# A four-stage transformer block on one core: other buffers and placements for the feed-forward halves, the distances of the first attention and the projections

## The chip, the core and the metric

The kernel runs on one core of a Trainium2 chip. A core has five engines with queues of their own: PE (TensorE, matmuls into PSUM), DVE (VectorE), ACT (ScalarE), POOL (GpSimd) and SP (SyncE, which here issues all DMAs). They meet through semaphores alone, and each takes its instructions strictly in the order in which they are written. The metric is device time in microseconds.

## The reference

The input x is 8 x 1024 x 256, float32. Four layers follow each other, each a residual one over a layer norm (LN):

```python
x = x + attn_a(layernorm(x))   # distance attention
x = x + ffn(layernorm(x))
x = x + attn_b(layernorm(x))   # softmax attention, 16 heads of 16
x = x + ffn(layernorm(x))

# attn_a: V = LN @ wv.T + bv; pos = LN @ w3d.T + b3d          (three coordinates)
#         attn = softmax over k of -|pos_q - pos_k| / 4, causal, the same for all heads
#         out = (attn @ V) @ wo.T + bo
# attn_b: k, q, v = LN @ Wkqv + bkqv; softmax(q k / 4), causal; out = attn @ v
# ffn:    x_prev = x one token back (zero at the first)
#         xr = mu_r * x + (1 - mu_r) * x_prev;  xk likewise
#         out = sigmoid(xr @ W_r.T) * (relu(xk @ W_k.T) ** 2 @ W_v.T)
```

## The kernel before

The program has one backbone and work hung beside it. The backbone is the second attention (att3). A batch element has 4 groups of 4 heads, a group has 12 pieces, a piece has 4 quarters, one for each head: 48 quarters a group, 192 an element (TURN). In quarter u (`pe_att3`, L797 to L841) PE computes one scores piece into one of two max_banks (L811), from which DVE takes the row maxima (L867 with the causal mask, L870 without), and, for the piece 14 slots (56 quarters) earlier, the transposed scores into one of two exp_banks (L822), which ACT exponentiates into pt (L852). POOL clears the part above the diagonal (L889), and once in four quarters PE multiplies with the values into o_bank (L837). At a group's end the maxima go through a side bank and a DMA back into the stack (L910, L920, L929), and halves of the output go through ot, a transposition (L944), a division (L954, L958) and an addition on POOL (L968).

The scores need exact products, so keys and queries are split into three bfloat16 parts, stored to DRAM (L702) and loaded back as stacks ks and qs, nine DMAs a group (L772). The first group of an element can be loaded once all eight parts of that element are stored.

Everything else is a stage: `att1` (first attention), `ffn2`, `proj3` (keys, queries and values of the second attention), `ffn4`. Each stage has an LN for each half h of 512 tokens. STAGES gives a starting quarter to every stage; offsets inside a stage come from JOBS and from `at(...)`. In turn n - 1 of the backbone the stages att1, ffn2 and proj3 of element n run, and ffn4 of element n - 2. All side jobs of PE use three PSUM banks (side): `place()` walks through the quarters, gives each job a bank and a quarter (PARTS_AT), and the quarter where it is emptied (EMPTIED_AT); where no bank is free the job is late, and all later ones keep that shift, which falls by one for 4 quarters. `WRITTEN_AT` applies the same shift to what is placed by `at`. `schedule` then writes, for each engine, the instructions quarter by quarter: those of att3 first, then those of the stages in the order of their start. A quarter is thus an order, no time; an engine that waits holds up all that is written behind it.

The first attention (att1): values with positions (L516, L389), positions turned into rows (L524, L439), then 12 pieces of distances: squares of three coordinate differences on ACT (L451), sums on POOL (L505) and DVE (L405), logarithm and two exponentials on ACT (L465, L468, L473), a select on POOL (L494), and one attend job for each tile of queries (L544) with the division and the residual on DVE (L412, L415). PIECE_TIME gives the quarters of a piece. In `dve_att1` residual and distance share one list: the residual that is due at a piece stands before that piece's L405.

The feed-forward halves: difference to the previous token on POOL (L559), two mixes on DVE (L582, L589), keys (L644), relu (L610), square (L567), receptance (L658), the sigmoid as exponential, logarithm, exponential on ACT (L619, L623, L626), products (L658), multiplication (L599), addition (L572). Their buffers are borrowed: xr, xk, ka lie in pb, kr and th in sq, both buffers of the distances. So ffn2 of an element waits for its last distance (L556, p1_exp), and the distances of the next element wait for the last feed-forward half (tm_ready). Both halves of a stage follow each other, since the second needs the first's last token, which lies beside it in xt.

An LN is statistics on DVE (L330, L337, L340), a power on POOL (L347), four normalisations on POOL (L353), transpositions on PE (L379) and copies to xt on ACT (L368). proj3 has eight projections (L718) into x32 (L687), split by DVE (L671, L674, L678) and POOL (L694).

Before quarter 0 stand the stages of element 0 (FIRST), where nothing of att3 runs beside them.

## Time and profile before

| | us |
|---|---|
| median of 3 runs | 2153.86 (2149.85 to 2161.84) |
| the profiled execution | 2155.86 |
| its span | 2154.1 |
| granted TensorE clock, mean | 0.941 of full speed |

The 2 us between the span and the time lie outside the instructions. The span falls into a prologue up to the first scores matmul (201.9 us), turns 0 to 7 of att3's 192 quarters, and a drain after the last scores matmul (2063.6). The windows of the rows below are cut at the scores matmul that begins a turn, or a stretch of quarters in a turn; those inside a turn are of turn 4, which begins at 1161.6 us. A busy engine is one with an instruction running; two that overlap count once, so the mean duration of an instruction times its count can be more than the busy time.

### The profile page before, as it was taken

To read this page: it belongs to the slowest core of one execution; us is meant where nothing else is said; L and a number is where in the kernel's file an instruction comes from. 1 tells how busy PE (TensorE), PEld (TensorE's weight loads), DVE (VectorE), ACT (ScalarE), POOL (GpSimd) and SP (SyncE) were. 2 spreads that over 40 slices of the span, in tenths; PEclk is the share of its full clock that TensorE was granted. 3 is DMA by queue.
4 is the path that set the end of the run, shared out by engine and by line. 5 is a ranking of instruction groups with operands and counts; after the bars stand their busy time and mean duration, and the time that the engine had idled before them with its cause. 6 is when DMAs were issued, how large, how long until landed. Compare 5 with 4: busy or idle time off the path is not lost. (4 is left out here: it accounts for less than half of the span.)

```text
span 2154.1 us, 32514 instructions
## 1 busy us (share of the span) xinstructions
PE 1852.8 (86%) x9842; PEld 921.0 (43%) x9842; DVE 1427.4 (66%) x4173; ACT 1245.4 (58%) x2673; POOL 1027.3 (48%) x1074
## 2 busy tenths in 40 slices
PE   4476799889998899988998899978998899988986
PEld 3344344434543355434544345424554345323423
DVE  2235767766786677776776676776876677777732
ACT  0722655685648655595557755495557756465562
POOL 4364254436662465435753366534753357314314
PEclk8778699999999999999999999999999999999988
DMA  3006010211223111311123111311123102322000
GB/s 103 1 8 140 1 31 23 67 30 30 40 88 60 31 30 55 74 31 30 41 74 74 30 21 49 89 31 30 31 77 79 24 11 40 98 47 44 1 21 20
DMA packets 64348, 97.27 MB, mean 45 GB/s; under 512 B 15656, under 2 KB 58030, under 8 KB 58031
## 3 DMA queue, kind: packets, MB, share of 16 engines
q1 hardware_dynamic: 64174, 95.20, 20.1%
q8 instruction: 80, 1.31, 0.3%
q14 instruction: 94, 0.76, 0.1%
HBM read 61.09 MB, written 33.55 MB: 44 GB/s over the span
## 5 line engine op out<-in xcount | busy, mean ns | idle before, releaser
L852 ACT ACTIVATE pt<-exp_bank 128x512 f32<-128x512 f32 (+3 forms) x1536 | 748.2, 496 | 664.7 <-PE exp_bank L822 657.5
L867 DVE CUSTOM_DVE_ANT_0 max_bank<-max_bank,mask 128x128 f32<-128x128 f32 (+3 forms) x1024 | 501.4, 501 | 402.1 <-PE max_bank L811 387.7
L811 PE MATMUL max_bank<-ks,qs 96*128 96x512 bf16 (+3 forms) x1536 | 517.9, 342 | 81.4 <-DVE piece_max L870 45.0
L822 PE MATMUL exp_bank<-qs,ks 98*128 98x512 bf16 (+3 forms) x1536 | 512.6, 340 | 69.2 <-ACT pt L852 67.0
L870 DVE TENSOR_REDUCE piece_max<-max_bank 128x1 f32<-128x512 f32 x512 | 343.5, 685 | 105.6 <-PE max_bank L811 102.3
L837 PE MATMUL o_bank<-pt,v 128*17 128x512 f32 (+3 forms) x3072 | 335.6, 510 | 7.6 <-ACT pt L852 3.1
L353 POOL TENSOR_SCALAR xh<-xs,mv,rstd 128x256 f32<-128x256 f32 x256 | 321.2, 1261 | 10.0 <-PE side L379 3.8
L811 PEld LDWEIGHTS max_bank<-ks,qs 96*128 96x128 bf16 x1536 | 150.6, 98 | 382.7 <-DVE piece_max L870 136.5
L889 POOL TENSOR_SCALAR_AFFINE_SELECT pt<-pt 128x512 f32<-128x512 f32 x256 | 170.4, 666 | 291.6 <-ACT pt L852 291.3
L822 PEld LDWEIGHTS exp_bank<-qs,ks 98*128 98x128 bf16 x1536 | 151.9, 100 | 281.4 <-ACT pt L852 174.6
L505 POOL TENSOR_TENSOR sq<-sq 128x512 f32<-128x512 f32 (+1 forms) x96 | 95.9, 999 | 230.1 <-ACT sq L451 230.1
L544 PE MATMUL side<-vp,p 128*128 128x260 f32 x576 | 169.6, 419 | 29.2 <-ACT p L473 19.5
L451 ACT ACTIVATE sq<-pb,neg_pos 128x512 f32<-128x512 f32 (+3 forms) x288 | 179.9, 627 | 2.4 <-ACT p L473 0.4
L644 PE MATMUL side<-pb,wkT 128*128 128x512 f32 x256 | 146.5, 664 | 9.7 <-DVE pb L582 9.6
L867 DVE DVE_READ_ACCUMULATOR2_ANT piece_max<- 128x1 f32 x1024 | 144.5, 141 | 0.0
L968 POOL TENSOR_TENSOR xs<-xs,on 128x256 f32<-128x256 f32 x64 | 49.4, 772 | 186.6 <-DVE on L958 186.6
L544 PEld LDWEIGHTS side<-vp,p 128*128 128x128 f32 x576 | 107.9, 203 | 68.3 <-ACT p L473 34.6
L718 PE MATMUL side<-xt,wkq 128*128 128x512 f32 x256 | 135.4, 615 | 1.5 <-DVE v L743 0.8
L559 POOL TENSOR_TENSOR pb<-xt 128x512 f32<-128x512 f32 x64 | 66.2, 1042 | 143.9 <-PE side L658 123.9
L658 PE MATMUL side<-wrT,pb 128*128 128x256 f32 x512 | 133.9, 387 | 0.0
L658 PE MATMUL side<-wvT,pb 128*128 128x256 f32 x512 | 133.1, 386 | 0.0
L379 PE MATMUL side<-ident,xh 128*128 128x128 f32 x512 | 84.1, 292 | 53.8 <-POOL xh L353 48.5
(94 smaller groups left out, 2284.0 us busy)
## 6 DMA issues: line engine op xcount, KB each, us to landing
parts_dram<-parts SPq DMA_DIRECT2D x64, 384.0 KB, 2.6
qs<-parts_dram SPq DMA_DIRECT2D x192, 128.0 KB, 7.1
ks<-parts_dram SPq DMA_DIRECT2D x32, 384.0 KB, 4.7
xs<-in_L_attn_a_x_dram SPq DMA_DIRECT2D x16, 512.0 KB, 4.2
ks<-parts_dram SPq DMA_DIRECT2D x32, 256.0 KB, 5.4
out_dram<-xs SPq DMA_DIRECT2D x16, 512.0 KB, 3.0
ks<-parts_dram SPq DMA_DIRECT2D x32, 128.0 KB, 5.9
qs<-neg_maxT SPq DMA_DIRECT2D x64, 8.0 KB, 1.9
```

Source lines behind the costliest of these rows:

```text
L353: pool.tensor_scalar(xh[:, t, :], src[:, TPH * h + t, :], mv[:, r, t, 0:1], rstd[:, r, t:t + 1], ALU.subtract, ALU.mult).then_inc(xh_ready, 1)
L451: mm = act.activation(sq[:, p % 2, c, 0:w], pb[:, c, q0:q1], ACT.Square, bias=neg_pos[:, kt, c:c + 1])
L544: mm = pe.matmul(bank[:, 0:VC], p1[:, at:at + P], vp[:, kt, :], start=(kt == 0), stop=(kt == t))
L644: mm = pe.matmul(bank[:, :], wkT[:, c, P * j:P * (j + 1)], xk[:, c, :], start=(c == 0), stop=(c == NC - 1))
L658: mm = pe.matmul(bank[:, C * t:C * (t + 1)], lhs[:, c, P * (2 * j + t):P * (2 * j + t + 1)], rhs[:, c, :], start=(c == 0), stop=(c == NC - 1))
L811: pe.matmul(max_bank[u % MAX_BANKS][:, 0:k1 - k0], qs[r][0:KROWS, j, P * tile:P * (tile + 1)], ks[r][0:KROWS, j, k0:k1], start=True, stop= ...
L822: pe.matmul(exp_bank[k % EXP_BANKS][:, 0:q1 - q0], ks[r][:, j, P * kt:P * (kt + 1)], qs[r][:, j, q0:q1], start=True, stop=True).then_inc(s ...
L837: mm = pe.matmul(o_bank[32 * j:32 * j + VW, q0 - HALF * h:q1 - HALF * h], v3[n % 2][:, kt, GH * (g % NG) + j, :], pt[:, (e - 1) % 2, j, 0: ...
L852: act.activation(pt[:, e % 2, j, 0:q1 - q0], exp_bank[k % EXP_BANKS][:, 0:q1 - q0], ACT.Exp, scale=SCALE).then_inc(exp_done, 1)
L867: dve.tensor_tensor_reduce(scores, scores, mask[:, HALF - w:HALF], 1.0, LOWEST, ALU.add, ALU.max, piece_max[:, j, m:m + 1]).then_inc(max_f ...
L870: dve.tensor_reduce(piece_max[:, j, m:m + 1], scores, AX.X, ALU.max).then_inc(max_free, 1)
L889: pool.affine_select(out=block, in_=block, compare_op=ALU.is_ge, fill=0.0, base=0, pattern=[[0, GH], [1, P]], channel_multiplier=-1).then_ ...
```

## The change

- xk, xr, ka and th become buffers of their own; kr and tm are gone (relu writes ka, the square and the product are done in place). x32 and parts move into p1 instead, so the projections wait for p1's last attend matmul, and p1's first exponential of the next element for the stored parts. ot has one buffer.
- ffn2 and ffn4 alternate by halves: ffn4 0, ffn2 0, ffn4 1, ffn2 1 at quarters 38, 56, 74, 92 of a turn (before 82, 50, 98, 66). ACT keeps the last column of each first half in `edge` and puts it back before the second half.
- The distances take 80 quarters (8 for a piece of 512) instead of 60. In `dve_att1` values, distances and residuals become three lists, so a distance no longer stands behind a residual.
- Projections and values of proj3 get quarters of their own (PROJECT_AT, VALUES_AT), in two groups of four.
- For element 0 DVE normalises in POOL's place.
- A delay falls by one for 3 quarters.

```diff
-ATT1, FFN2, FFN4, PROJ3 = -44, 50, 82, 114
-FIRST = {("att1", 0): -220, ("ffn2", 0): -126, ("proj3", 0): -74,
-         ("att1", 1): -28, ("ffn2", 1): 66, ("proj3", 1): 114}
+STARTS = {("att1", 0): -36, ("att1", 1): -24, ("ffn4", 0): 38, ("ffn2", 0): 56, ("ffn4", 1): 74, ("ffn2", 1): 92,
+          ("proj3", 0): 108, ("proj3", 1): 138}
+HEAD = -200
-LN_HALF = {"att1": 8, "ffn2": 16, "ffn4": 16, "proj3": 12}
...
-PIECE_TIME = [2 + (q1 - q0) // P for _, q0, q1 in KEY_PIECES] + [5, 5, 5]
-PIECE_AT = [34 + sum(PIECE_TIME[:p]) for p in range(NP + 4)]
+PIECE_TIME = [{P: 4, 2 * P: 5, 3 * P: 7, 4 * P: 8}[q1 - q0] for _, q0, q1 in KEY_PIECES] + [5, 5, 5]
+PIECE_AT = [32 + sum(PIECE_TIME[:p]) for p in range(NP + 4)]
...
+PROJECT_AT = [18, 22, 26, 30, 46, 49, 52, 55]
+VALUES_AT = [34, 37, 57, 59]
...
-            regained = max(0, shift - max(0, at - before) // 4)
+            regained = max(0, shift - max(0, at - before) / REGAIN)
...
-        xr, xk, ka = (pb[:, k, :].rearrange("p (c n) -> p c n", c=NC) for k in range(3))
-        kr = sq[:, 0, 0:2, :]
-        th = sq[:, 1, 0:2, :].rearrange("p a (b c) -> p (a b) c", c=C)
-        tm = sb("tm", [P, TPH, C])
-
-        x32 = sb("x32", [P, 2, HALF])
-        parts = sb("parts", [P, 2, 3, HALF], BF16)
+        xk, xr, ka = (sb(name, [P, NC, HALF]) for name in ("xk", "xr", "ka"))
+        th = sb("th", [P, TPH, C])
+        edge = sb("edge", [P, 2, NC, 1])
+
+        x32 = p1[:, 0:2 * HALF].rearrange("p (r n) -> p r n", r=2)
+        parts = p1[:, 2 * HALF:5 * HALF].bitcast(BF16).rearrange("p (r k n) -> p r k n", r=2, k=3)
...
+            if n > 0:
+                return
+            for t in range(TPH):
+                yield at(7 + t)
...
+                dve.tensor_scalar(xh[:, t, :], src[:, TPH * h + t, :], mv[:, r, t, 0:1], rstd[:, r, t:t + 1],
+                                  ALU.subtract, ALU.mult).then_inc(xh_ready, 1)
...
+                    if h == 1 and s in ("ffn2", "ffn4"):
+                        act.wait_ge(edge_kept, EDGE_AT[s, n] + 1)
+                        act.activation(last, kept, ACT.Copy).then_inc(edge_put, 1)
...
+            if h == 0 and s in ("ffn2", "ffn4"):
+                act.wait_ge(xt_ready, 2 * q + 2)
+                act.activation(kept, last, ACT.Copy).then_inc(edge_kept, 1)
...
-                    if s == "ffn2":
-                        pool.wait_ge(p1_exp, NP * (n + 1))
                     if f > 0:
                         pool.wait_ge(r_full, 2 * f)
+                    if h == 1:
+                        pool.wait_ge(edge_put, EDGE_AT[s, n] + 1)
...
                 if f > 0:
-                    act.wait_ge(ka_ready, 2 * f - 1 + j)
-                act.activation(kr[:, j, :], side_of("keys", s, n, h, j)[:, :], ACT.Relu).then_inc(kr_ready, 1)
+                    act.wait_ge(v_full, 2 * f)
+                act.activation(ka[:, j, :], side_of("keys", s, n, h, j)[:, :], ACT.Relu).then_inc(kr_ready, 1)
...
-                        act.wait_ge(tm_ready, 2 * f - 1 + j)
+                        act.wait_ge(x_added, 2 * f - 1 + j)
...
+                if j == 0:
+                    act.wait_ge(pv1_full, 8 * (n + 1))
```

Three places show how the order moves. First POOL in the prologue, from the end of the distances of element 0 to its projections. xh is the normalised half, pb (xr after) the difference, pb<-sq (ka<-ka after) the square, xs the addition, parts (p after) the split of a projection. Before:

```order
L347 TENSOR_TENSOR rstd<-var_eps,minus_half 128x4
L353 TENSOR_SCALAR xh<-xs,mv,rstd 128x256 x4
L567 TENSOR_TENSOR pb<-sq 128x512 x2
L559 TENSOR_TENSOR pb<-xt 128x512 x2
L572 TENSOR_TENSOR xs<-xs,tm 128x512 x2
L567 TENSOR_TENSOR pb<-sq 128x512 x2
L572 TENSOR_TENSOR xs<-xs,tm 128x512
L347 TENSOR_TENSOR rstd<-var_eps,minus_half 128x4
L572 TENSOR_TENSOR xs<-xs,tm 128x512
L353 TENSOR_SCALAR xh<-xs,mv,rstd 128x256 x4
```

After:

```order
L590 TENSOR_TENSOR xs<-xs,th 128x512
L579 TENSOR_TENSOR xr<-xt 128x512 x2
L362 TENSOR_TENSOR rstd<-var_eps,minus_half 128x4
L585 TENSOR_TENSOR ka<-ka 128x512 x2
L712 TENSOR_TENSOR p<-p 128x512
L590 TENSOR_TENSOR xs<-xs,th 128x512 x2
L712 TENSOR_TENSOR p<-p 128x512 x3
L362 TENSOR_TENSOR rstd<-var_eps,minus_half 128x4
L712 TENSOR_TENSOR p<-p 128x512 x4
```

The normalisations are gone from POOL, and the first split of a projection stands ahead of the second half's last additions.

Second DVE in a turn, where the last distance piece (L405, L435 after, 128 columns) meets the residual of a tile (L412 and L415, L445 and L448 after). L867 and L885 are maxima of att3. Before, at quarter 53:

```order
L867 ISA max_bank,piece_max<-max_bank,mask 128x256
L867 ISA piece_max 128x1
L412 RECIPROCAL rinv<-side 128x1
L415 SCALAR_TENSOR_TENSOR xs<-side,rinv,xs 128x256
L405 SCALAR_TENSOR_TENSOR sq<-sq 128x128
L330 BN_STATS st<-xs 128x6
```

After, at quarters 81 and 82:

```order
L435 SCALAR_TENSOR_TENSOR sq<-sq 128x128
L335 BN_STATS st<-xs 128x6
L885 ISA max_bank,piece_max<-max_bank,mask 128x128
L885 ISA piece_max 128x1
L445 RECIPROCAL rinv<-side 128x1
L448 SCALAR_TENSOR_TENSOR xs<-side,rinv,xs 128x256
```

The distance stands ahead of the residual, and 28 quarters later.

Third PE near a turn's end, at the last projection of an element (L718, L736 after), whose parts the next turn's stack is made from. L732 and L750 are values of proj3, L811 and L829 the scores. Before, 31 and 30 quarters ahead of the turn:

```order
L718 MATMUL side<-xt,wkq 128x512
L811 MATMUL max_bank<-ks,qs 128x512
L822 MATMUL exp_bank<-qs,ks 128x256
L944 MATMUL side<-ident,ot 128x128 x4
L718 MATMUL side<-xt,wkq 128x512
```

After, 21 and 20 quarters ahead:

```order
L736 MATMUL side<-xt,wkq 128x512
L829 MATMUL max_bank<-ks,qs 128x512
L840 MATMUL exp_bank<-qs,ks 128x512
L736 MATMUL side<-xt,wkq 128x512
L829 MATMUL max_bank<-ks,qs 128x512
L840 MATMUL exp_bank<-qs,ks 128x512
L750 MATMUL side<-wv,xt 128x256 x2
```

The last projection stands 10 quarters nearer to the scores that need it, and the values follow it.

## Rows read from the trace of the kernel before

**Rows 1.** The page, busy time of the engines with its share of the span.

```profile
PE 1852.8 (86%) x9842; PEld 921.0 (43%) x9842; DVE 1427.4 (66%) x4173; ACT 1245.4 (58%) x2673; POOL 1027.3 (48%) x1074
```

**Rows 2.** Windows, us and busy (x count) of PE, PEld, DVE, ACT, POOL; clock, DMA.

```profile
0.00:201.90 201.90, 116.85 (x418) 82.66 (x419) 69.95 (x190) 63.00 (x119) 98.46 (x98) 0.81 0.23 57
201.90:424.20 222.30, 194.23 (x964) 94.95 (x963) 162.04 (x484) 127.08 (x265) 93.52 (x97) 0.90 0.18 38
...
1161.60:1407.70 246.10, 223.19 (x1229) 111.64 (x1225) 176.02 (x519) 153.93 (x336) 127.10 (x132) 0.97 0.21 48
...
1890.80:2063.60 172.80, 150.86 (x899) 56.24 (x895) 125.82 (x379) 100.44 (x219) 52.24 (x62) 0.96 0.16 29
2063.60:2154.10 90.50, 63.84 (x296) 28.24 (x296) 18.25 (x44) 37.17 (x81) 33.96 (x36) 0.79 0.07 24
```

**Rows 3.** Windows of turn 4: quarters 0-48, 48-72, 72-96, 144-192, 156-168.

```profile
1161.60:1213.90 52.30, 41.94 (x236) 15.88 (x233) 35.93 (x107) 49.23 (x112) 19.39 (x27) 0.93 0.18 31
1213.90:1243.20 29.30, 24.13 (x153) 13.41 (x151) 19.82 (x70) 12.33 (x35) 13.38 (x18) 0.99 0.27 55
1243.20:1278.10 34.90, 34.60 (x169) 16.37 (x166) 23.88 (x66) 19.73 (x37) 22.94 (x22) 0.91 0.01 2
1343.30:1407.70 64.40, 59.37 (x330) 30.34 (x328) 50.40 (x148) 33.93 (x71) 29.94 (x28) 1.00 0.33 83
1359.50:1375.70 16.20, 15.31 (x84) 7.57 (x83) 16.06 (x41) 7.61 (x18) 13.05 (x13) 1.00 0.22 74
```

**Rows 4.** Turn 4: waits of ACT (sum, times, longest), timelines of ACT and PE.

```profile
ACT sq L465 <- DVE sq L405: 8.0, 5, 4.2
...
1222.61 0.31 ACT L465 ACTIVATE sq<-sq 128x128 f32<-128x128 f32 x1 [4.17 <-DVE sq L405]
...
1223.25 0.23 PE L822 MATMUL exp_bank<-qs,ks 98*128 98x128 bf16 x1 [2.09 <-ACT pt L852]
```

**Rows 5.** Chain (start, us, what), ACT's timeline, groups by line (busy us, mean ns).

```profile
1989.79 0.87 PE side L658 x4
...
1222.83 0.53 ACT L852 ACTIVATE pt<-exp_bank 128x256 f32<-128x256 f32 x2
...
L451 ACT ACTIVATE sq<-pb,neg_pos 128x512 f32<-128x512 f32 (+3 forms) x288 | 179.9, 627 | 2.4 <-ACT p L473 0.4
L465 ACT ACTIVATE sq<-sq 128x512 f32<-128x512 f32 (+1 forms) x96 | 50.9, 530 | 73.9 <-DVE sq L405 73.5
```

**Rows 6.** Timelines of the prologue, ACT, DVE and POOL.

```profile
58.38 1.37 ACT L451 ACTIVATE sq<-pb,neg_pos 128x512 f32<-128x512 f32 x2
...
106.58 0.48 DVE L415 SCALAR_TENSOR_TENSOR xs<-side,rinv,xs 128x256 f32<-128x256 f32 x1
...
112.45 5.67 POOL L353 TENSOR_SCALAR xh<-xs,mv,rstd 128x256 f32<-128x256 f32 x4
...
139.68 4.84 POOL L353 TENSOR_SCALAR xh<-xs,mv,rstd 128x256 f32<-128x256 f32 x4
...
181.13 1.15 POOL L694 TENSOR_TENSOR parts<-x,parts 128x512 bf16<-128x512 f32 x1 [2.61 <-DVE parts L678]
```

**Rows 7.** SP's timeline ahead of turn 4; the page's landing time.

```profile
1135.63 0.36 SPq L702 DMA_DIRECT2D parts_dram<-parts  x1
...
1139.58 2.73 SPq L772 DMA_DIRECT2D qs<-parts_dram  x6
...
qs<-parts_dram SPq DMA_DIRECT2D x192, 128.0 KB, 7.1
```

**Rows 8.** Groups of the whole span, and a wait of POOL (sum, times, longest).

```profile
L330 DVE BATCH_NORM_STATS2 st<-xs 128x6 f32<-128x256 f32 x256 | 104.8, 417 | 5.3 <-POOL xs L968 3.4 <-POOL xs L572 1.7
...
POOL pb L559 <- PE side L658: 123.9, 21, 7.0
...
L837 PE MATMUL o_bank<-pt,v 128*17 128x512 f32 (+3 forms) x3072 | 335.6, 510 | 7.6 <-ACT pt L852 3.1 <-POOL pt L889 2.2 <-ACT ot L937 2.1
```

190 lines of the change are left out of this document (98 added, 92 removed).

## The prediction

> **What bounds the kernel now.** I read the time by turn first. A turn is one batch element's 192 quarters; a quarter is one scores matmul with its maximum, and one exponential. Before the first quarter lie 201.9 us, the last two rows are turn 7 and the drain, and the turns between repeat at 246 us [rows 2]. By the page PE is busy 86% of the span [rows 1], so PE looks like the bound. Inside a turn that isn't so [rows 3]: in its first 48 quarters (52.3 us) ACT is busy 49.2 and PE 41.9; in the second half of the next 48 PE is busy 34.6 of 34.9, in the last 48 it is busy 59.4 of 64.4, with DVE at 16.1 of 16.2 us in one piece of it. So the bound changes hands: ACT while the distances of the first attention run, PE with DVE later. Work is bunched, and a turn costs the sum of each stretch's worst engine. That is what the change can move; almost nothing is added or removed.
>
> Busy PE isn't PE at its rate either. Four records of a 256-column matmul take 0.87 us when they run behind each other [rows 5], 0.22 each. Counted by such rates (a 512-column score product 0.22, an f32 matmul of 256 columns in two records 0.44, a transposition 0.11), a turn holds some 195 us of PE work, against 223 busy. The Trainium skill ("Perfetto Trace Analysis", Identifying the Most-Contended Engine) says as much: matmul busy time is a poor measure of headroom. By busy time a turn could give 23 us at most, by columns 51; the trace sides with columns, and the sum below doesn't rest on that sentence.
>
> **The change, part by part: the steady turns (1 to 5).** I counted from the two orders what each engine has in each group of 48 quarters, and priced it by rows.
>
> Quarters 0 to 48. On ACT the distance operations fall from 60 to 42 (squares 30 to 23, the other three 30 to 19); 5 position copies and 1 transposed copy come in. Squares at 0.627 and the others at 0.53: -7 x 0.627 - 11 x 0.53 = -10.2; +6 x 0.60 = +3.6 [rows 5]. That is -6.6, or -5.3 where starts stand 0.1 closer than durations, as in the row of two exponentials in 0.53. ACT is busy 94% of this stretch, so most of it counts; but PE gains 3.0 of columns (values and positions enter, 5 attend matmuls leave), and quarters 12 to 24 get heavier on ACT. I take -4; bounds -6.6 and 0.
>
> Quarters 48 to 96. Now 29.3 and 34.9 us [rows 3]. The first half holds a stall: ACT's L465 waits 4.17 us for DVE's L405, and PE's L822 stands 2.09 us for ACT [rows 4]. L405 stands on DVE behind the residual L415, which waits for an attend matmul that PE issues slowly among the scores. ACT's five such waits in a turn sum to 8.0 us; I take 3 us of the turn's time for them. After, the distances are a list of their own and stand ahead of the residuals, and there are 8 quarters to a piece of 512 instead of 6, so the stall goes. Next late there is ACT with 20 us and DVE with 20. That half falls by about 5. The second half gets denser: 22 attend matmuls (0.44) come in, 16 transpositions (0.11) and 4 key matmuls (0.86) leave: +4.4, its columns go from 29.7 to 34.1. Before, 34.9 us held 29.7 of columns, 3.3 of them lost to a clock of 0.91; the rest is a ratio of 1.06. 34.1 x 1.06 + 3.3 = 39.5: +4.6. Together -0.5; bounds -5 and +5.
>
> Quarters 96 to 144 lose 0.9 of PE columns at an even load: -1. Quarters 144 to 192: columns -3.4 (16 position transpositions and 8 value matmuls leave, 8 LN transpositions and 4 others enter), ACT -4.8, and the 12 quarters where DVE was the worst engine (16.1 us) hold 12 of it after. The pieces' worst engines sum to 57.8 before and 51.6 after; the row is 64.4. I take -4.5; bounds -6.5 and -1.
>
> A turn: -4 - 0.5 - 1 - 4.5 = -10, to 236. Five turns: -50. Turn 0 (222.3) is the same by these counts: 0. Turn 6 has half the moved work, -3; turn 7 only an ffn4 that comes 44 and 24 quarters earlier, -2.
>
> **The stack that comes later.** x32 and parts now lie in p1, free only once p1's last attend is done (placed 30 quarters ahead: 0), and the projections sit at other quarters. The last part of an element is stored 13 quarters before its scores start, before it was 22. By rows: issued 1135.6, the last of the stack's nine DMAs issued at 1142.3, landing a median 7.1 us after issue: 1149.4 [rows 7], 13.8 us after the store; the scores begin at 1161.6 [rows 2]. So 12 us were spare. 9 quarters later at 1.1 us is 10 us of it, and the issue itself followed its quarter by 2.6 us before. I expect PE to wait 0 to 4 us on the stack, six times (elements 2 to 7): +1.7 each, +10; bounds 0 and +30. Queued behind that wait are all scores and side jobs of PE, hence ACT and DVE.
>
> **The prologue (201.9 us).** For element 0 the normalisation moves from POOL to DVE: four in 4.84 us against 4 x 0.42 by the statistics on the same 128x256 operand [rows 6, 8], -3.1 a half. Where it is on the path: both halves before the first square (58.38), which also no longer stands behind positions 3 to 5 and values 4 to 7: -7. The second feed-forward half ran from the last residual (107.1) to its last addition (139.7), with LN at 5.67 beside the first half's matmuls; now the first half is under way during the distances: -8. From 139.7 to the last part (182.3) both projection LNs and all eight projections ran; now half 0's are placed ahead of it, so one LN and four projections remain: -18 of 42.6. Sum -33. The lower end is the LN swap alone, three exposures, -9. In-order queues will not overlap that well, so I take -25. From the last part to the first score lie POOL's two LNs of the next element (4.84 and more each) and the DMA's 14: unchanged.
>
> **Small items.** 32 ACT copies of one column (under 0.27 us each, a 256-column exponential's share of a row of two [rows 5]) lie beside PE work: 0, up to +3. Sharing th and ka between halves adds waits: relu waits for the previous half's products, the sigmoid for its addition; both are placed 4 or more quarters earlier, so 0. POOL's wait for the receptance, 123.9 us in 21 times [rows 8], stays at three a turn. One ot buffer waits for a transposition 32 quarters back: 0. Drain: +1.
>
> **Sum.** -50 - 3 - 2 + 10 - 25 + 1 = -69 on the profiled execution's 2155.9: 2087. The median of the runs shown is 2 us lower, so 2085.
>
> **Rivals.** *Prologue only as the LN swap* (its chain is held by ACT's 12 pieces and by queue order): -9 for -25: 2101. For it: 48.7 us lie between the first square and the last residual [rows 6], most of them ACT's own distance work, whatever is placed beside it. *The stack is late by the whole lag:* +5 a turn instead of 1.7: 2105. For it: the spare of 12 us is nearly gone; against: POOL's queue ahead of the last part is shorter. *The dense half eats the gain:* 34 us of columns in 24 quarters behind 24 that hold only 18, with the clock at 0.91 there already [rows 3]: 3.3 us, a stretch of some 7 us at the lower of its two levels (1.2 for 2.4 GHz). Were that stretch 17 us, it would cost 8: +5 a turn, 2085 + 30 = 2115. The Trainium skill ("TensorE: Matmul & The Clock Gate", Part 1) has the clock fall after an idle stretch, and PE is thinnest here in quarters 48 to 60; by its rule the fall would move to quarter 60. *Slower:* POOL waits for the receptance up to 7.0 us at a time [rows 8]. If the interleaved halves put its selects and additions behind such a wait while DVE now needs the output addition at once (ffn4's first half starts at quarter 38, where that addition stands), each of three places a turn could cost 6 us: 18 x 6 = 108, less 69: 2194. It decides from 4 us a place. Against: today the selects aren't late by it, o_bank's matmuls wait 2.2 us for them in the whole span [rows 8]. *Doesn't do what it says:* turns stay at 246 because latency, not load, sets them: 2085 + 50 = 2135 with the prologue's gain.
>
> **How the numbers follow.** Forecast 0.54, prologue smaller 0.10, stack 0.10, dense half 0.10, no gain in the turns 0.08, slower 0.08. Below the forecast's centre the bounds (-6.6, -5, -6.5 in the stretches, -33 in the prologue, no wait) would reach 2025 if all held at once; half of that way, 2050, I take as the low end; to hold 8 in 10 the range goes up over the first three rivals with some slack: 2050 to 2125. A measurement here tells 0.5% (11 us) from no change. Faster than 2143: 0.87 (it takes in most of the case without gain in the turns). Within: 0.06. Slower: 0.07.
>
> **What would show it.** First score at 175 to 180 us in place of 201.9. Turns of 234 to 238. ACT's share of quarters 0 to 48 under 90%, and that stretch under 49 us. No ACT wait of over 2 us for the distance scalar on DVE. At each turn's start a PE wait for a DMA of ks or qs of 0 to 4 us. A clock below 0.9 in quarters 60 to 84. I'm wrong if turns stay at 246, if DVE waits for POOL's addition at quarter 38, or if the first score stays near 200.

## The result and the profile after

The changed kernel took 2264.67 us (median of four runs) against 2153.38 us of the kernel before: a ratio of 1.051, 95% interval 1.048 to 1.055. It is 5% slower, where 2085 was forecast.

The page of the changed kernel, busy time of the engines, as [rows 1]:

```profile
PE 1905.6 (84%) x9842; PEld 947.5 (42%) x9842; DVE 1456.4 (64%) x4205; ACT 1259.2 (56%) x2705; POOL 989.7 (44%) x1042
```

Each engine's share of the span is as it was or lower. The windows of prologue, turn 0, turn 4 and turn 7, with the columns of [rows 2]:

```profile
0.00:195.90 195.90, 117.07 (x431) 84.43 (x432) 79.29 (x215) 66.71 (x127) 69.97 (x75) 0.83 0.25 62
195.90:427.00 231.10, 198.28 (x940) 93.54 (x939) 160.41 (x479) 122.24 (x256) 91.15 (x97) 0.85 0.16 34
1211.90:1474.60 262.70, 230.72 (x1226) 115.23 (x1224) 179.12 (x519) 156.12 (x338) 127.88 (x133) 0.94 0.20 45
1995.00:2174.00 179.00, 152.87 (x894) 56.82 (x894) 124.96 (x376) 101.15 (x221) 51.25 (x61) 0.95 0.15 28
```

The prologue gives 6 us back. Turn 0 is 9 us longer, the five steady turns together 81 (turn 4: 262.7 for 246.1), turn 6 20, turn 7 6, and the drain 1 shorter: 109 us, the difference of the spans. Nearly all of it is in the turns. By 48 quarters, turn 4 was 52.3, 64.1, 65.3, 64.4 and is 50.7, 71.2, 74.9, 66.0: the loss lies in quarters 48 to 144, for which the forecast had -1.5.

Windows inside turn 4 after, as [rows 3]: quarters 0-48, 48-60, 60-72, 108-120, 144-192.

```profile
1211.90:1262.60 50.70, 42.03 (x257) 18.22 (x255) 37.00 (x116) 43.89 (x98) 17.83 (x24) 1.00 0.19 32
1262.60:1279.60 17.00, 11.41 (x62) 4.30 (x58) 7.86 (x31) 9.77 (x24) 10.02 (x10) 0.61 0.27 55
1279.60:1297.00 17.40, 16.57 (x76) 6.79 (x77) 13.39 (x32) 11.28 (x28) 13.88 (x15) 0.79 0.22 39
1351.10:1374.60 23.50, 18.29 (x88) 9.34 (x84) 11.86 (x31) 8.55 (x22) 13.49 (x13) 0.85 0.21 46
1408.60:1474.60 66.00, 57.56 (x311) 28.50 (x310) 51.69 (x151) 30.65 (x63) 36.26 (x35) 0.97 0.28 73
```

In quarters 48 to 60 no engine is busy for more than 11.4 of 17.0 us, and the clock is 0.61. In quarters 108 to 120 PE is busy 18.3 of 23.5. Nobody is full there, so somebody waits. The waits of PE in turn 4 after (sum, times, longest):

```profile
PE side L405 <- POOL xh L370: 9.3, 3, 4.9
PE max_bank L829 <- DVE piece_max L885: 8.3, 15, 1.8
PE max_bank L829 <- DVE piece_max L888: 3.8, 8, 1.1
```

L405 are the transpositions of the normalised rows (L379 before), L370 is the normalisation on POOL (L353 before), the two others are maxima. The first of the long waits, in POOL's and PE's timeline of the changed kernel around quarter 50 (ffn4's first half; its statistics end at 1257.87 on DVE):

```profile
1257.70 0.17 DVE L345 TENSOR_SCALAR var_eps<-mv 128x4 f32<-128x4 f32 x1
...
1259.20 0.63 POOL L907 TENSOR_SCALAR_AFFINE_SELECT pt<-pt 128x512 f32<-128x512 f32 x1 [2.92 <-ACT pt L870]
...
1259.80 1.46 POOL L362 TENSOR_TENSOR rstd<-var_eps,minus_half 128x4 f32<-128x4 f32 x1
...
1261.37 3.64 POOL L370 TENSOR_SCALAR xh<-xs,mv,rstd 128x256 f32<-128x256 f32 x3
...
1263.83 0.27 PE L840 MATMUL exp_bank<-qs,ks 98*128 98x256 bf16 x1
...
1264.96 0.64 POOL L907 TENSOR_SCALAR_AFFINE_SELECT pt<-pt 128x512 f32<-128x512 f32 x1
...
1265.56 1.26 POOL L522 TENSOR_TENSOR sq<-sq 128x512 f32<-128x512 f32 x1
...
1266.81 1.22 POOL L370 TENSOR_SCALAR xh<-xs,mv,rstd 128x256 f32<-128x256 f32 x1
...
1268.09 1.12 PE L405 MATMUL side<-ident,xh 128*128 128x128 f32 x4 [3.98 <-POOL xh L370]
```

From the end of the statistics to the fourth normalised tile 10.2 us pass on POOL: 1.9 before it starts, behind a selection that waited for ACT, and 1.9 for a selection and a distance sum ahead of the fourth tile. The transpositions stand 6 quarters behind the normalisation, and a quarter takes 1.0 us here (quarters 36 to 48 took 12.1 us). So PE, which issues in order, stands for 3.98 us with all scores behind it. At quarter 113 (ffn2's second half) it is the same, with an addition and a square of the half before and a selection between POOL's four tiles:

```profile
1363.02 1.11 PE L405 MATMUL side<-ident,xh 128*128 128x128 f32 x4 [4.86 <-POOL xh L370]
```

Three windows, the first of them still in the first wait, show the second price, the granted clock (column before the DMA share):

```profile
1265.60:1268.60 3.00, 0.51 (x3) 0.52 (x4) 0.00 (x0) 0.00 (x0) 2.43 (x3) 0.64 0.00 0
1268.60:1283.60 15.00, 12.96 (x56) 4.38 (x55) 10.32 (x35) 10.56 (x25) 6.08 (x7) 0.50 0.55 107
1283.60:1286.60 3.00, 3.00 (x12) 0.41 (x10) 2.75 (x8) 1.60 (x4) 2.90 (x4) 0.50 0.05 8
```

PE had been idle for 4 us, and the clock fell in that wait; then PE runs 18 us at the lower level, 1.2 GHz. The Trainium skill ("TensorE: Matmul & The Clock Gate", Part 1) has the clock fall after idleness; the trace agrees.

**An account of a turn.** I cut turn 4 of each kernel into 16 windows of 12 quarters and took from each PE's busy time, its idle time (length less busy) and the clock's loss (busy x (1 - clock)). Busy less loss is work at full clock. "Floor" is the sum over the 16 windows of the largest of PE's work at full clock and the busy times of DVE, ACT and POOL.

```
us in turn 4            turn   work at full clock   idle   clock's loss   floor
before                  246.1        217.3          22.9        5.9        228.4
after                   262.8        217.2          32.0       13.6        228.3
```

Work and floor are the same to 0.1 us. The change flattened nothing, taken over the turn: by 48 quarters the floor was 49.2, 55.9, 63.2, 60.1 and is 47.0, 60.1, 62.8, 58.5, so what the first and the last stretch gave the second took. The 16.7 us are 9.1 of standing and 7.7 of lower clock. The profiles of two runs below, e9 and e11, were taken at a lower clock throughout (0.73 as a mean, and 0.95 where others show 1.00; e11's four times reach from 2129 to 2161 us), so their turns are not split in this way.

### The profile page after: what moved, and what is told of

The parts are those of the page before. It is cut to its first block and busy times, and to the rows that moved or that the text cites. A ratio compares the mean times of both kernels' runs of the same rounds, so it can differ in the third digit from the quotient of the medians.

```text
span 2263.2 us, 32530 instructions
## 1 busy us (share of the span) xinstructions
PE 1905.6 (84%) x9842; PEld 947.5 (42%) x9842; DVE 1456.4 (64%) x4205; ACT 1259.2 (56%) x2705; POOL 989.7 (44%) x1042
## 5 line engine op out<-in xcount | busy, mean ns | idle before, releaser
L870 ACT ACTIVATE pt<-exp_bank 128x512 f32<-128x512 f32 (+3 forms) x1536 | 738.4, 492 | 809.9 <-PE exp_bank L840 799.7
L885 DVE CUSTOM_DVE_ANT_0 max_bank<-max_bank,mask 128x128 f32<-128x128 f32 (+3 forms) x1024 | 499.5, 500 | 412.7 <-PE max_bank L829 404.5
L829 PE MATMUL max_bank<-ks,qs 96*128 96x512 bf16 (+3 forms) x1536 | 532.3, 351 | 117.4 <-DVE piece_max L885 76.4
L840 PE MATMUL exp_bank<-qs,ks 98*128 98x512 bf16 (+3 forms) x1536 | 521.4, 344 | 18.7 <-ACT pt L870 16.4
L855 PE MATMUL o_bank<-pt,v 128*17 128x512 f32 (+3 forms) x3072 | 349.1, 529 | 3.2 <-POOL pt L907 2.0
L829 PEld LDWEIGHTS max_bank<-ks,qs 96*128 96x128 bf16 x1536 | 153.0, 100 | 456.7 <-DVE piece_max L885 249.0
L370 POOL TENSOR_SCALAR xh<-xs,mv,rstd 128x256 f32<-128x256 f32 x224 | 283.0, 1271 | 5.1 <-PE side L405 1.2
L405 PE MATMUL side<-ident,xh 128*128 128x128 f32 x512 | 97.7, 326 | 126.2 <-POOL xh L370 81.0
L660 PE MATMUL side<-xk,wkT 128*128 128x512 f32 x256 | 144.1, 652 | 10.9 <-DVE xk L600 9.7
L674 PE MATMUL side<-wrT,xr 128*128 128x256 f32 x512 | 141.8, 404 | 9.4 <-ACT xt L391 7.2
L736 PE MATMUL side<-xt,wkq 128*128 128x512 f32 x256 | 138.8, 631 | 6.5 <-ACT xt L391 6.5
L885 DVE DVE_READ_ACCUMULATOR2_ANT piece_max<- 128x1 f32 x1024 | 143.6, 140 | 0.6
L405 PEld LDWEIGHTS side<-ident,xh 128*128 128x128 f32 x512 | 70.9, 167 | 161.6 <-POOL xh L370 96.7
L674 PE MATMUL side<-wvT,ka 128*128 128x256 f32 x512 | 133.2, 385 | 3.5 <-DVE xs L448 3.5
```

What stands on the lines that cost most here:

```text
L370: pool.tensor_scalar(xh[:, t, :], src[:, TPH * h + t, :], mv[:, r, t, 0:1], rstd[:, r, t:t + 1], ALU.subtract, ALU.mult).then_inc(xh_ready, 1)
L405: mm = nc.tensor.transpose(bank[:, P * t:P * (t + 1)], xh[:, t, P * c:P * (c + 1)], ident[:, :])
L674: mm = pe.matmul(bank[:, C * t:C * (t + 1)], lhs[:, c, P * (2 * j + t):P * (2 * j + t + 1)], rhs[:, c, :], start=(c == 0), stop=(c == NC - 1))
L829: pe.matmul(max_bank[u % MAX_BANKS][:, 0:k1 - k0], qs[r][0:KROWS, j, P * tile:P * (tile + 1)], ks[r][0:KROWS, j, k0:k1], start=True, stop= ...
L840: pe.matmul(exp_bank[k % EXP_BANKS][:, 0:q1 - q0], ks[r][:, j, P * kt:P * (kt + 1)], qs[r][:, j, q0:q1], start=True, stop=True).then_inc(s ...
L855: mm = pe.matmul(o_bank[32 * j:32 * j + VW, q0 - HALF * h:q1 - HALF * h], v3[n % 2][:, kt, GH * (g % NG) + j, :], pt[:, (e - 1) % 2, j, 0: ...
```

## The experiments

Labels e1 to e18; "turn" is turn 4. The times of all, beside the kernel before in the same chip job (idle and clock's loss by the account above):

```
run                        us     ratio (interval)          turn   idle  loss
e1 vector norm, 2 halves   2217   1.029 (1.026 to 1.032)    256.6  28.9  10.2
e2 fillers                 2236   1.037 (1.035 to 1.038)    258.2  25.8   6.1
e3 old table               2159   1.001 (0.999 to 1.002)    250.3  24.8   7.5
e4 before + lists          2127   0.986 (0.984 to 0.987)    242.3  20.0   6.0
e5 e1 and e2 together      2260   1.048 (1.047 to 1.050)    259.2  28.3   4.7
e6 old table, diffs later  2140   0.993 (0.991 to 0.995)    246.2  22.6   6.1
e7 e1, distances in 60     2252   1.045 (1.043 to 1.046)    262.3  35.0   9.6
e8 e4 + first image        2125   0.986 (0.984 to 0.987)    242.8  21.0   4.7
e9 vector norm, 6 halves   2207   1.020 (1.017 to 1.022)
e10 vector norm, 1 half    2240   1.035 (1.032 to 1.038)    260.1  32.8   9.9
e11 e8 + fillers           2136   0.990 (0.983 to 0.996)    249.5
e12 two halves 3 later     2305   1.066 (1.064 to 1.069)    272.4  36.4  20.9
e13 vector norm, all 8     2197   1.017 (1.011 to 1.023)    256.0  29.1   8.7
e14 differences 2 later    2281   1.057 (1.051 to 1.063)    262.5  35.7  10.0
e15 e8 + one in three      2160   0.999 (0.996 to 1.002)    249.2  21.4  12.3
e16 e15 + att1's h1        2160   1.001 (0.999 to 1.003)    249.2  21.2  12.2
e17 e8 + att1's h1         2115   0.980 (0.978 to 0.983)    242.5  18.1   9.1
e18 transposes 1 later     2245   1.040 (1.037 to 1.043)    261.7  29.4  16.0
```

Work at full clock is 215 to 218 in all but e2 and e5, which hold fillers (226).

**The late normalisation.** e1 moves the four tiles of two halves from POOL to DVE; POOL keeps the power. In effect:

```
# dve_statistics (and the reverse in pool_normalise)
-            if n > 0:
+            if n > 0 and (s, h) not in (("ffn4", 0), ("ffn2", 1)):
                 return
```

> The changed kernel, with the four normalise instructions of two halves a turn (ffn4's first, ffn2's second) on VectorE instead of GpSimd: 4 x 0.46 us (VectorE's rate in the first image) for 4 x 1.27 us. Theory 1 (GpSimd is late with the normalisation of these two halves; TensorE waits 4.0 us at quarter 50 and 4.9 us at quarter 113, and the clock of 0.61 to 0.79 and 0.85 behind the waits costs some 5 to 8 us more): both waits fall under 1 us, a turn goes from 262.9 to 246 to 252 us, the time to 2165 to 2200 us. Theory 2 (the turn is long because distances and feed-forward halves lie beside each other in quarters 48 to 144, and the waits only stand where the lateness comes out): a turn stays above 258 us, the time above 2235 us.

2217 us, 47 less, between the theories, and so is the turn (256.6). In turn 4 of e1, quarters 48-60, 60-72 and 108-120:

```profile
1244.20:1257.60 13.40, 9.87 (x63) 3.71 (x60) 9.99 (x37) 9.32 (x23) 6.90 (x7) 0.78 0.28 59
1257.60:1275.00 17.40, 16.93 (x81) 7.13 (x78) 12.96 (x31) 11.51 (x28) 13.30 (x15) 0.78 0.28 48
1329.10:1348.40 19.30, 15.86 (x88) 7.60 (x85) 15.50 (x35) 8.64 (x22) 8.92 (x9) 1.00 0.28 56
```

17.0 became 13.4 and 23.5 became 19.3: the late rows cost these two stretches 3.6 and 4.2 us, wait and clock together. PE's wait at quarter 113 is still 1.6 us, now for DVE, and the one at quarter 159 grew from 0.4 to 2.1 us. The clock falls all the same in the thin quarters 48 to 60, and quarters 60 to 72 stay at 17.4. e10 takes one half alone:

> The changed kernel with the normalisation of ffn4's first half alone on VectorE (quarter 50's wait of 4.0 us, and the clock behind it). With both halves moved a turn lost 6.2 us: quarters 48 to 72 lost 3.8, quarters 108 to 120 lost 4.2. If the two waits are independent: quarters 48 to 72 at 30 to 32 us, quarters 108 to 120 still 23.5, a turn 258 to 260 us, the time 2232 to 2245 us. If the first wait's gain is taken again further on: over 2255 us.

2240, within: the first half alone is worth about 25 us, and the second 22 more once the first has moved.

**Wait and clock apart.** e2 leaves the wait and gives PE something to do in it:

```
 # pe_transposed, c == 0 of the same two halves
+                    for k in range({("ffn4", 0): 4, ("ffn2", 1): 5}[s, h]):
+                        nc.tensor.matmul(bank[:, :], ident[:, :], mask[:, :], start=True, stop=True)
                 nc.tensor.wait_ge(xh_ready, TPH * (q + 1))
```

> The changed kernel, with idle matmuls (128x512, 4 before ffn4's first half, 5 before ffn2's second) put into the bank of the transposes right before TensorE's wait for the normalised rows; the waits' ends don't move. It separates the wait from the clock. If the low clock behind the waits (0.61 and 0.79 in quarters 48 to 64) comes from TensorE standing still in the wait: the clock of that stretch rises to over 0.9 and a turn goes from 262.9 to 255 to 259 us, the time to 2220 to 2245 us. If the clock is low because that whole stretch has little TensorE work (or costs nothing, as TensorE isn't the last there): the turn stays within 1.5 us, the time at 2255 to 2275 us.

2236: the first case. The four fillers (two records each) in quarter 50 of e2, and the windows 48-60 and 60-72:

```profile
1249.99 3.60 PE L405 MATMUL side<-mask,ident 128*128 128x512 f32 x8
...
1248.60:1262.60 14.00, 10.98 (x70) 4.47 (x67) 7.42 (x31) 8.93 (x22) 10.32 (x11) 1.00 0.23 45
1262.60:1279.30 16.70, 15.60 (x77) 6.88 (x77) 13.32 (x32) 11.89 (x29) 13.53 (x16) 0.90 0.33 60
```

The clock stands at 1.00 and 0.90 for 0.61 and 0.79. 28 us of the 111 are a price of the clock that 9 useless matmuls a turn buy back. e5 has both edits:

> Both edits of the two runs before in the changed kernel: the normalisation of two halves on VectorE and the 4 and 5 idle matmuls ahead of their transposes. If wait and clock are two costs, the clock's being what is left of the long quarters 48 to 72 once the wait is gone (17.4 us for quarters 60 to 72 with a clock of 0.78): quarters 48 to 72 go from 30.7 to 26 to 28 us, a turn from 256.6 to 252 to 254 us, the time to 2190 to 2205 us. If the fillers helped only because TensorE was waiting anyway: they now cost their own time, 1 to 3 us a turn, 2217 to 2235 us.

2260, a clear miss, worse than even the bad case; every turn but the last is 2 to 6 us longer than in e1, the last 9, the drain 7. In turn 4 the clock's loss is 5.5 us less, but PE's work is 8.7 us more. Quarters 108 to 120 take 22.7 us with PE busy 20.1, against 19.3 and 15.9 in e1: where the wait is short, fillers are work, 0.9 us each on the queue that everything waits for. In e2 most of their time lay in a wait: PE's idle time there is 6.2 us less than in the changed kernel.

**The plan's distance between rows and transpositions.** e12 moves all of the two halves that follows the normalisation by 3 quarters, e18 only the transpositions of three halves by one (both edits shortened):

```
e12  + LATER = {("ffn4", 0): 3, ("ffn2", 1): 3}     # added to the half's jobs and its steps on POOL, DVE, ACT
e18  - jobs = [((name, s, n, h, k), *when) for name, k, *when in JOBS["ln"]]
     + jobs = [((name, s, n, h, k), at + ((s, h) in (("ffn2", 1), ("ffn4", 0), ("proj3", 1))), *when) ...
```

> The changed kernel, where everything of ffn4's first and ffn2's second half behind the normalisation (transposes, differences, products, additions) stands 3 quarters later; the normalisation stays on GpSimd and where it was. No work moves to another engine. Theory 1 (TensorE comes to the transposes before GpSimd has the rows, so 12 quarters between statistics and transposes are too few where quarters take 1 us): both waits fall to 0 to 1.5 us, a turn from 262.9 to 252 to 258 us, the time to 2190 to 2235 us. Rival (the waits only moved: GpSimd is late by as much as its queue is long): the waits stay over 3 us, 2250 to 2275 us.

> The changed kernel with only the transposes of three halves (ffn4's first, ffn2's second, the third attention's second) set one quarter later, so that they stand 7, 6 and 6 quarters behind the normalisation instead of 6, 5 and 5. Moved on with them by the plan: the third attention's projections by 1 to 2 quarters, the first attention's values by 2. Theory (quarters between rows and transposes too few): each wait shortens by about the quarter, 1.0 to 1.5 us each with less clock loss, 3 to 6 us a turn, 2225 to 2248 us. Rival (a quarter more changes nothing as everything behind moves too, and the stack, which had 2.3 us to spare, is now waited for): 2258 to 2285 us.

e18: 2245, 20 us less, as the theory had it, though this profile's turn 4 saved only 1.1 us (the others up to 4.1) and 7 us of the gain lie in prologue and drain. PE's waits for rows went from 9.3 to 6.2 us a turn: 3.98 became 0.9, 4.86 became 2.3, but the third, 0.42, became 2.9, although it too had a quarter more. e12: 2305, worse than either expectation. ffn2's second half is followed by the projections of the third attention and these by the stack. Two of PE's three longest kinds of wait in e12, from the start of turn 4 to that of turn 5, both included:

```profile
PE max_bank L840 <- DMA qs<-parts_dram: 10.3, 2, 5.5
...
PE side L413 <- POOL xh L378: 8.0, 3, 3.3
```

The stack is waited for at the start of each of turns 2 to 7, 4.0 to 7.2 us; in the changed kernel there were some 3 us to spare at turn 4's. So that half can't be given its time back. The waits for rows are at quarters 53 (2.4 us), 134 (2.4) and 165 (3.3). The quarters in the plan say why the first is left: `place()` and `WRITTEN_AT` pass the delay on from turn to turn, so in e12 the normalisation of ffn4's first half moved too, from 44 to 47, and its transpositions from 50 to 53. The distance stayed 6; e12 tests what it was meant to test in ffn2's second half alone (111, 120: 9), and there the wait is gone. Normalisation (its power), transpositions, and what lies between, for five halves of a turn:

```
half (turn)            before             after            e15
ffn4 first             88,  94:  6        44,  50:  6
ffn4 second           104, 110:  6        87,  96:  9
ffn2 second            72,  78:  6       108, 113:  5
third att. second     132, 139:  7       154, 159:  5
first att. second     166, 172:  6       182, 188:  6      166, 171: 5
```

In the changed kernel PE waits for rows at the two halves with 5 (4.86 and 0.42 us) and at the one with 6 in the fast quarters (3.98 us), and nowhere else in the turn; in the kernel before only at the first attention's second half (1.3 us). The distance alone does not give the size of a wait: what else stands on POOL, and how late PE itself comes, count too, as the third wait of e18 shows.

**Delays made up sooner, alone.** e15 is e8 (below) with the plan's lag made up one quarter in three instead of four. In a turn of the plan this moves 17 PE jobs of the first attention forward by 1 or 2 quarters, and by as much the steps of the other engines that `at` places from quarter 164 of a turn to quarter 6 of the next; no other PE job.

```
-            regained = max(0, shift - max(0, at - before) // 4)
+            regained = max(0, shift - max(0, at - before) / 3)      # and the same in WRITTEN_AT, rounded up
```

> The kernel before with split lists and the first image's normalisation on VectorE (2125 us), and delays of the plan made up one quarter in three instead of one in four. Halves of the feed-forward and projections come some quarters sooner behind a shift. Neutral, as the prediction had it (priced at 0): 2120 to 2130 us. If it brings halves onto each other as in the changed kernel: over 2135 us.

2160 for 2125. Quarters 168-180 of e15, and 0-12, where the clock is lowest:

```profile
1377.70:1399.90 22.20, 18.31 (x94) 10.02 (x93) 11.18 (x29) 8.53 (x15) 7.15 (x7) 0.85 0.51 108
...
1164.70:1178.30 13.60, 13.04 (x67) 5.86 (x64) 7.32 (x32) 9.99 (x28) 3.67 (x9) 0.63 0.49 86
```

By the account idle time grew by 0.4 us in the turn and the clock's loss by 7.6, while work fell by 1.5. One or two quarters less for these steps cost 1.6%. e16 takes the rows of that half off POOL:

> The kernel before with split lists, the first image's normalisation on VectorE and delays made up one in three (2160 us), and the normalisation of the first attention's second half on VectorE. That rule brought the transposes of this half from quarter 172 to 171, 5 quarters behind its normalisation instead of 6; the turn grew from 242.8 to 249.2 us, with TensorE waiting 1.8 us for the rows and 1.8 us more for the first values, and clock below. Theory (one quarter too few for GpSimd's 5.1 us of rows, and the clock behind the wait): with 1.8 us of rows on VectorE the wait goes, the turn is back at 241 to 245 us, the time at 2115 to 2135 us. Rival (the other jobs that came 1 or 2 quarters sooner are the cause): 2150 us or more.

2160: the rival's case, and my theory in its narrow form falls. The wait for rows is gone and another stands in its place, the first values of the second half waiting for ACT's copy of the transposed rows, which also sits a quarter closer. PE's timeline of e15, then of e16:

```profile
1385.01 0.66 PE L392 MATMUL side<-ident,xh 128*128 128x128 f32 x4 [1.78 <-POOL xh L366]
...
1389.94 2.10 PE L534 MATMUL side<-wvp,xt 128*128 128x259 f32 x4 [1.79 <-ACT xt L381]
```

```profile
1387.94 1.14 PE L539 MATMUL side<-wvp,xt 128*128 128x259 f32 x4 [2.21 <-ACT xt L386]
```

So a faster normalisation wins nothing of the 35 us of e15 back. That the cause is any step whose producer is placed too few quarters ahead is my reading; the 17 jobs were not moved one by one, and which of them costs isn't shown.

**How far it goes in the changed kernel.**

> The changed kernel with the normalisation of all feed-forward and third-attention halves (of the images after the first) on VectorE, six halves a turn instead of two. The waits that are left in the run with two halves moved are partly of the same kind (TensorE's transposes of the second third-attention half still wait 2.1 us for GpSimd's normalised rows). Theory 1 (late normalisation, anywhere): a turn goes from 256.6 to 250 to 255 us, the time from 2217 to 2175 to 2210 us. Rival (VectorE, whose instructions stand in the way of its own maxima, is as late as GpSimd was): 2215 us or more.

> The changed kernel with every normalisation on VectorE (the first attention's too, eight halves a turn). With six halves on VectorE the time was 2207 us, but that profile had a clock of 0.73 throughout and can't be read. This one adds the first attention's halves at quarters 156 to 180, where VectorE is busy 16.9 of 18.4 us. If late rows from GpSimd were all that keeps the turn above 246 us: 2150 to 2180 us. If VectorE pays for the two halves in its full stretch: 2205 to 2225 us, quarters 168 to 192 longer than 33.4 us, while no wait of TensorE for normalised rows is over 1.5 us anywhere.

2207, within; 2197, between the two cases of its expectation. With all rows on DVE, PE's wait for rows in turn 4 falls from 9.3 to 2.1 us, and 68 of the 111 us come back. Idle time is still 29.1 us, against 20 in e4: what is left is spread, and the largest item is PE waiting for maxima, 14.7 us in e13 (two kinds, 10.0 and 4.7) against 7.7 in e4. DVE is busy 192 us of the turn then, for 179:

```profile
1181.50:1437.50 256.00, 226.87 (x1227) 113.01 (x1226) 192.38 (x551) 156.02 (x338) 89.36 (x101) 0.96 0.20 46
```

> The changed kernel with the differences xr on GpSimd two quarters later (18 and 19 behind the half's start instead of 16 and 17). With the old table one quarter was worth 20 us, as the differences waited for the half before with selections of pt queued behind them. Theory A (the same in the new table: GpSimd waits up to 5.6 us at the differences, and the selections behind them, and so TensorE's output products, are late): 2 to 4 us a turn, 2240 to 2252 us. Theory B (in the new table TensorE doesn't wait for these selections, its waits are for normalised rows): 2258 to 2275 us.

2281, worse than both. The same step that pays in the old table (e6) costs in the new one. Turn 4 is no longer (262.5 us), turns 0 and 2 are 2 and 3 us longer and turn 7 is 7; why isn't shown.

**Buffers and table.** e3 puts the table of before (starts, pace, projections, one in four) back into the changed kernel; e6 also sets the differences back to their old quarter.

```
# e6, pool_ffn
-                yield at(16 + c)
+                yield at(17 + c)
```

> The changed kernel with the table of before (starts of the stages, 60 quarters for the distances, times of projections and values, regained one quarter in four); its own buffers, separate lists, kept edges, single ot and the first image's normalisation on VectorE stay. Theory 1 (the table crowds GpSimd, the buffers are harmless): the time is that of the kernel before less what the lists and the first image give, 2130 to 2155 us, a turn 243 to 247 us. Rival (the changed buffers bring waits of their own, the aliases of p1 and the single ot above all): over 2190 us.

> The changed kernel with the old table once more, and the differences xr of a feed-forward half on GpSimd one quarter later, as in the kernel before (17 and 18 quarters behind the half's start instead of 16 and 17). With the old table the two differences stand ahead of two diagonal selections of pt in GpSimd's queue and hold them while they wait up to 7 us for the receptance products of the half before; TensorE's output products wait for the selections, 1.9 and 1.4 us in quarters 96 to 120. If that is the 33 us that the old table with the changed buffers is slower than the old kernel with the lists split: quarters 96 to 120 go from 34.3 to 31.1 us, the time from 2159 to 2135 to 2145 us. If it is the buffers: 2155 to 2163 us.

2159 and 2140. The quarters 96-120 of e3, then of e6:

```profile
1274.10:1308.40 34.30, 30.08 (x176) 17.66 (x175) 25.21 (x71) 18.39 (x44) 21.36 (x23) 1.00 0.26 48
```

```profile
1265.80:1297.30 31.50, 30.03 (x177) 17.63 (x176) 23.34 (x69) 18.39 (x44) 19.95 (x21) 1.00 0.27 52
```

In e3 this was two waits of PE's output products for selections that stood on POOL behind the differences, 3.3 us in all. So the table, with its rule of one in three and its quarter for the differences, costs 2265 - 2140 = 125 us, and the buffers with all the rest cost 15 against e8, whose cause I did not follow (its quarters 0 to 12 and 144 to 168 are the longer ones).

e7 is e1 with the old pace of 60 quarters; the new starts stay:

> The changed kernel with the normalisation of two halves on VectorE, and the distances at the pace of before (60 quarters instead of 80); the starts of the stages stay. The spread over 80 quarters puts the last attend products and residuals beside the first feed-forward half. If the spread costs (the products leave the stretch of low clock, quarters 60 to 72): that stretch goes from 17.4 to 13 to 15 us and quarters 0 to 48 from 51.5 to 52.5, the time from 2217 to 2185 to 2205 us. If the spread saves, as the prediction had it (4 us a turn in quarters 0 to 48, where ScalarE is full): 2230 to 2250 us.

2252 for 2217: the spread of the distances over 80 quarters saves 34 us, given the new starts. That is the part of the change that does what the prediction said: quarters 0 to 48 take 51.7 us in e1 and 54.7 in e7, 3.0 for the 4 forecast. The rest of the 34 us was not in the forecast.

**The parts that were right, alone.** e4 splits DVE's list of the first attention in three, in the kernel before (shortened):

```
-            for p in range(NP + 3):
-                for t in range(NT):
-                    if attended_from(t) == p:
-                        yield EMPTIED_AT["attend", "att1", n, 0, t]
-                        residual(t)
-                if p < NP:
-                    yield at(PIECE_AT[p + 1])
-                    distance(p)
+            return [all_values(), distances(), residuals()]     # three lists, each with its own quarters
```

> The kernel before with only VectorE's list of the first attention split in three (values, distances, residuals), so that distances are issued at their own quarter and no longer behind a residual. The prediction's step: the stalls of ScalarE for distances (3 us a turn) go, six turns, 2153 to about 2135 us. Rival (another engine is as late there): 2148 to 2158 us.

2127, a ratio of 0.986, 8 us better than expected. Quarters 48 to 60, in the kernel before and in e4:

```profile
1213.90:1231.40 17.50, 14.45 (x89) 9.24 (x88) 9.89 (x43) 6.64 (x20) 7.21 (x10) 1.00 0.29 61
...
1196.70:1210.80 14.10, 14.10 (x89) 9.36 (x88) 9.76 (x43) 6.68 (x20) 7.21 (x10) 1.00 0.37 70
```

PE has no gap in e4, and ACT's wait for the distances is 2.0 us a turn for 8.0. e8 adds the first image's normalisation on DVE, e17 that of the first attention's second half in every image, e11 instead a filler in five thin quarters:

> The kernel before with the split lists and the first image's normalisation on VectorE. The first score comes 4 to 8 us sooner (the changed kernel's first square came 7.5 us sooner), the turns stay at 242 us, the time from 2127 to 2118 to 2124 us. If the next late thing of the prologue takes the gain: 2125 to 2129 us.

> The kernel before with split lists, the first image's normalisation and that of the first attention's second half on VectorE; delays made up one in four as before (2125 us without the last edit). There TensorE waits 1.3 us a turn for these rows (quarter 172), of 2.3 us that it stands idle in quarters 168 to 180, and VectorE is busy 11.7 us of 19.3. By theory 1 to 2.5 us a turn: 2110 to 2119 us. If VectorE's queue there is as late: 2122 to 2130 us.

> The kernel before with split lists and the first image's normalisation on VectorE (2125 us), with one idle matmul of 128x256 in each of quarters 66 to 70 of a turn. There TensorE is busy 1.6 to 2.2 us of 3, and the clock falls to 0.50 for the 8 us behind it, in which TensorE has 2.7 to 3 us of work in 3 (3.2 us of a turn lost to the clock). If the idle matmuls keep the clock: 2.0 to 3.2 us a turn back less 0.5 to 1 for their own time, 2110 to 2118 us. If the clock falls all the same or the matmuls delay the scores: 2125 to 2135 us.

e8 2125, between its two cases: the first score comes at 190.1 us for 201.8, but turns and drain gave most of it back. e17 2115: the fastest of all, 2% under the kernel before. e11 2136, 1 us outside its second case: no gain, and the loss can't be sized with times that reach from 2129 to 2161 us. Its clock did not fall to 0.50 behind the thin quarters. Quarters 48 to 72 took 27.2 us for 25.7, but this profile's clock stood at 0.95 there for 1.00.

## Why the prediction was wrong

**The step that failed** is the first one: "a turn costs the sum of each stretch's worst engine. That is what the change can move." The floor of the account is that sum, 228.4 us before and 228.3 after, while the turn went from 246.1 to 262.8. Two things failed in it. Of the 10 us forecast for a turn, 3 were the stall and 7 were to come off that sum, which did not fall. And the prediction read the 17.7 us above the floor as if fixed but for the stall; they were waits and clock, and the change doubled them to 34.5. Of the 27 us by which the turn missed its forecast, 7 are the first and 20 the second (+17 where -3 was forecast). In its working no term is a distance between a producer's quarter and its consumer's, and delays made up sooner, the last item of the change's own list, were not priced at all (e15: 35 us, in the old table).

Term by term, turn 4, forecast and measured: quarters 0 to 48, -4 and -1.6 (the floor alone -2.2); 48 to 96, -0.5 and +7.1 (floor +4.2); 96 to 144, -1 and +9.6 (floor -0.4); 144 to 192, -4.5 and +1.6 (floor -1.6). In the second stretch the dense half's load came as forecast, +4.7 of floor for +4.6. The half before it was to fall by 5 and grew by 5, from 29.3 to 34.4 us, with ACT and DVE busy 21 us, close to the 20 forecast, and POOL, which the forecast did not name there, 23.9 for 13.4 before; none of them fills it. The last stretch was taken from the placed orders, 57.8 down to 51.6 of worst engines; the trace has 60.1 and 58.5, with DVE busy 51.7 us for 50.4, and PE idle 8.4 us for 5.0.

**The stall** of ACT for the distances: right, and of the right size. It fell from 8.0 to 1.2 us a turn, and e4 shows 3.8 us of turn 4 for the 3 forecast. The change bought this and lost it elsewhere.

**The clock**: right as a rival, mis-sized as a sum. "Were that stretch 17 us, it would cost 8" is what came: 18 us at the lower level, 8.0 us lost in quarters 48 to 72. The fall began at quarter 50, with the wait, and not at 60. The rival stopped there at +5 a turn, as it had no wait to go with it.

**The stack**: +10 forecast, 3 measured: PE waits for it once, 3.1 us at the start of turn 7. For turn 4 its last part is issued at 1195.0, its last DMA at 1201.7, and the first score has no wait. The last line is that of PE's waits of the whole span:

```profile
1195.01 0.36 SPq L720 DMA_DIRECT2D parts_dram<-p  x1
1197.65 1.25 SPq L790 DMA_DIRECT2D ks<-parts_dram  x3
1198.95 2.73 SPq L790 DMA_DIRECT2D qs<-parts_dram  x6
...
1211.88 0.22 PE L829 MATMUL max_bank<-ks,qs 96*128 96x128 bf16 x1
...
PE max_bank L829 <- DMA qs<-parts_dram: 3.1, 1, 3.1
```

With 7.0 us to landing it had 3 us to spare; e12 used them up. The slack was real, and nearly spent.

**The prologue**: -25 forecast, -6 measured, less than the rival's -9. The first square came 7.5 us sooner, as forecast (7):

```profile
50.88 1.33 ACT L469 ACTIVATE sq<-pb,neg_pos 128x512 f32<-128x512 f32 x2
...
106.09 0.48 DVE L448 SCALAR_TENSOR_TENSOR xs<-side,rinv,xs 128x256 f32<-128x256 f32 x1
...
141.33 1.65 POOL L590 TENSOR_TENSOR xs<-xs,th 128x512 f32<-128x512 f32 x1 [0.96 <-DVE th L615]
...
171.87 1.15 POOL L712 TENSOR_TENSOR p<-p 128x512 bf16<-128x512 f32 x1 [1.95 <-DVE p L694]
```

The last residual came only 0.5 sooner (106.6 for 107.1; between the two lie 55.7 us for 48.7, a stretch that the forecast took as unchanged), the last addition 3 us later (143.0 for 139.7), the last part 9 sooner (173.0 for 182.3), and from it to the first score 22.9 us passed for 19.6. The gains between those milestones were sized at 8 and 18 and came as -4 and 13. In the order POOL's steps for one half stand between those of the other; that this is what held the last addition was not tested.

**The slower rival** had the right kind (POOL late at three places a turn, PE standing) and the wrong object: selections and output additions, at 6 us a place. It was the normalised rows, at 4.0, 4.9 and less, and then the clock. In turn 4 DVE never waited for POOL's addition.

**Open.** With all normalisation off POOL the changed kernel stays 72 us above e8. The starts can't be tried one by one: ffn2's second half at 92 needs the third attention's at 138, and this the divided projections. So which of them scatters the rest of the waits isn't shown. Nor is it shown that short distances between producer and consumer explain more than the waits for rows: no run lengthened the distance of another step alone.

## What to carry to other kernels

In a kernel whose order is written out beforehand, list for every step of every queue how many slots lie between producer and consumer, times the length of a slot at that place, and compare with the producer's chain as it stands in the trace, other work on its queue included; a load table can't see what is lost there. Cut the turn into work at full clock, idle time and clock's loss before and after: when the first is the same, the engine shares say nothing. An in-order engine that stands for 4 us can cost it twice, once as a wait and once as clock behind it.

## What the runs showed of the hardware

A wait of PE of 3.98 us was followed by 18 us at 1.2 GHz, through windows in which PE was busy 12.96 of 15.0 and 3.0 of 3.0 us. In e1 the clock fell as well without the wait, in quarters where PE was busy 9.9 of 13.4 us. Idle matmuls of 128x512 (0.9 us each) held it at 0.90 to 1.00 in quarters 48 to 72, in e2 at a gain of 28 us and in e5 at a loss of 43. The same normalisation of a 128x256 tile takes 1.22 us on POOL and 0.41 on DVE (medians of the changed kernel and of e13).
